# A decoder layer with routed experts on one core: the second group's expert choice, ranks and places moved earlier in the hand-written order

## The chip, the cores and the metric

The kernel runs on one core of one Trainium2 chip. The metric is the device time of one execution in microseconds (us), lower is better. TensorE is called PE, VectorE DVE, ScalarE ACT, GpSimd POOL and SyncE SP.

## The reference

The input `x` is 32 sequences of 64 tokens, 128 wide, so 2048 tokens. Three steps follow one another, each with a residual and a layer norm.

```python
x = layernorm(x + attention(x))            # 16 heads, causal, with a null key and value
x = layernorm(x + cross(x, ctx))           # per sequence: mean correlation -> top 8 delays,
                                           # softmax weights, shifted values summed, @ Wo.T
logits = x @ Wr + br                       # 8 experts
idx, gate = argmax(logits), max(softmax(logits))
h = gelu(x @ W1[idx] + b1[idx])            # 128 -> 512, exact gelu
x = layernorm(x + gate * (h @ W2[idx] + b2[idx]))
```

Every token goes through one expert alone, so the kernel has to know a token's expert before it can do the last layer of that token.

## The kernel before, in words

The 2048 tokens are 16 tiles of 128. A loop over the 16 steps runs the attention: in step t PE makes the scores of tile t+1 (L535), turns the probabilities of tile t (`turn_probs`), multiplies tile t-1's by the values (`mix_values`, L566) and projects tile t-2 out (`project_out`, L585). ACT takes the turned tiles out of PSUM, DVE subtracts maxima, normalises tile t-1 (`normalize`, L1057) and adds the residual of tile t-2 (`residual`, L1070), POOL masks the keys and multiplies the null values.

The cross attention and the choice of expert go by groups of four tiles. The four groups are tiles 0 to 3, 4 to 7, 8 to 11 and 12 to 15; in the tail of the program three of them are `g1, g2, g3` (g1 is the second group). `WHOLE` is g2, `NT` is 16. A group passes through this sequence, with the engine and the line of each step:

- `variance` and `inverse_std` give the first norm's scale (DVE L1157, POOL L411); `scale_routed` (L269) applies it to the routing columns; `means` (PE L662), `subtract_mean_max` (DVE L1170) and `exp_means` (ACT L934) give the delay weights; `first_norm` (ACT L915) the normed rows.
- `weight_sums` (DVE L1178), `taps`, `permute` (DVE L1184) and `circulants` (L286, POOL for g0 to g2) make a 128x128 matrix of each tile; `mix_context` (PE L676) multiplies the context values by it, in two parts of two tiles, and `second_sum` (DVE L1188) adds the rows to each.
- `square_sums` (ACT L922) and `second_inverse_std` (POOL L416) give the second norm's scale, `second_norm` (ACT L928) its rows.
- `logits` and `pick` (DVE L1197 and L1207, seven small operations) find the expert; `exp_logits` (ACT L938, eight small instructions for a group) sums the exponentials. `ranks` (PE L686) counts, with small matmuls into PSUM, where in its expert's region each token goes; `place` (DVE L1223) turns that into a row number and `gates` (DVE L1219) makes the gate, one reciprocal.
- `scatter` (POOL L429) writes the tile's rows to DRAM, sorted by expert, one indirect DMA for each tile.

After the scatters of the first 12 tiles have landed (`scattered_first`), SP loads the first 5 of 23 slots of 128 sorted rows (L362), and the last stage begins: for each slot PE turns the rows and runs both layers of its expert (`up`, L830, and `down`, L846), ACT the gelu, DVE the norm, POOL an inverse root and an indirect DMA to the output.

No planner sets the order; each engine's program is an order written out by hand, with waits on semaphores. In step 15, the last of the loop, DVE does: `normalize(14)`, `weight_sums(g2)`, `permute(g2)`, `residual(13)`, `logits(g1)`, `pick(g1)` (L1318 to L1363). Behind the loop each engine has a written tail: DVE L1368 to L1398, PE L799 to L814, ACT L975 to L989, POOL L483 to L490. POOL's tail is: two scatters of g1, `inverse_std(g3)`, `second_inverse_std(g2)`, the other two of g1, four of g2, `second_inverse_std(g3)`, four of g3. ACT's begins with the copy of tile 14's turned attention (`take_attnT`, L889), `exp_logits(g1)`, `first_norm(g2)`, the copy of tile 15's, and `square_sums(g2)` in two parts. A scatter waits for its group's places, gates and normed rows:

```python
pool.wait_ge(S["slots_ready"], g.n + 1)
pool.wait_ge(S["gate_ready"], g.n + 1)
pool.wait_ge(S["x2_ready"], g.first + g.size)
```

Of the kernel before, what the change touches and what calls it, by code (L numbers as in the profile page):

```python
# [18 lines left out]
NT = B * T // P  # L19
# [57 lines left out]
GROUPS = [Group(0, 0, 4), Group(1, 4, 4), Group(2, 8, 4), Group(3, 12, 4)]  # L77
WHOLE = GROUPS[2]
# [10 lines left out]
def due(step, lag):  # L89

    return [g for g in GROUPS if g.ready + lag == step]


def due_mixed(step, lag):

    return [g for g in GROUPS if g.mixed_at + g.more + lag == step]
# [11 lines left out]

def chosen_in(step):

    return due_mixed(step, 1) if step < NT - 2 else due_mixed(step, 2) if step == NT - 1 else []


def placed_in(step):
# [9 lines left out]
def decoder_layer(nc, a, out):  # L124
    with ExitStack() as ctx:
# [383 lines left out]
        def _(pe):  # L509
# [68 lines left out]
            def turn_attn(t):  # L578
                pe.wait_ge(S["attn_ready"], t + 1)
                pe.wait_ge(S["v_ready"], min(t + 5, NT))  # L580
                if t >= 1:
                    pe.wait_ge(S["attnT_ready"], t)
                nc.tensor.transpose(attnT_ps, attn[:, t % 2, :], ident).then_inc(S["attnT_done"], 1)
# [92 lines left out]
            def mix_context(g, k, done):  # L676

                if alone(g.mixed_at) and k == 0:
                    pe.wait_ge(S["y2_a_ready"], g.n)
                pe.wait_ge(S["cw_ready"], -(-(g.first + g.size) // CHUNK))  # L680
                pe.wait_ge(S["circ_ready"], g.n + 1)
                for j, t in enumerate(range(g.part(k).start, g.part(k).stop)):
                    last = nc.tensor.matmul(mix_ps(g, k)[:, j * EXT:(j + 1) * EXT], circ[:, t, :], cw[:, t, :], start=True, stop=True)
                last.then_inc(S[done], 1)
# [29 lines left out]
            def sixth_bank_read(t):  # L714

                made = {0: ("folds1_ready", 4), 1: ("folds2_ready", 2), 2: ("sk_ready", 1), 3: ("x_route_ready", 1), 4: ("a_route_ready", 1),
                        5: ("bias_ready", 1)}
                if t in made:
                    name, count = made[t]
                    pe.wait_ge(S[name], count)  # L720
                if 1 <= t < NT + 1:
                    pe.wait_ge(S["attn_ready"], t)
                for g in due(t, 1):
                    pe.wait_ge(S["m_sub"], g.n + 1)
                for g in first_mixed_in(t):
                    pe.wait_ge(S["y2_a_ready"], g.n + 1)
                for g in second_mixed_in(t):
                    pe.wait_ge(S["y2_b_ready"], g.wide_before + 1)
                for g in placed_in(t):
                    pe.wait_ge(S["ranks_taken"], g.n + 1)  # L730
# [67 lines left out]

            g1, g2, g3 = BEHIND  # L799
            turn_attn(NT - 2)  # L800
            sixth_bank_read(NT - 1)
            mix_values(NT - 1)
            ranks(g1)
            project_out(NT - 2)
            mix_context(g2, 0, "mix_a_done")
            turn_attn(NT - 1)
            mix_context(g2, 1, "mix_b_done")
            project_out(NT - 1)
            means(g3)
            ranks(g2)  # L810
            mix_context(g3, 0, "mix_a_done")
# [205 lines left out]
        def _(dve):  # L1017
# [283 lines left out]
            for t in range(NT):  # L1301
                for g in due(t, 2):
                    if t < NT - 1:
                        weight_sums(g)
                        permute(g)
                if t + 3 < NT:
                    rope(t + 3)
                if t == 2:
                    dve.wait_ge(S["late_consts_in"], 16)
                    v.tensor_copy(tri_b, const("earlier"))  # L1310
                    v.memset(ones_f[:, :], 1.0)
                    v.memset(jump_base[:, :], float(REGION))
                    v.memset(ones_b, 1.0)
                    v.tensor_copy(region_b.rearrange("p (t e) -> p t e", e=E), const("region_part").unsqueeze(1).to_broadcast([P, 4, E])).then_inc(S["ranks_in"], 1)
                if t + 1 < NT:
                    subtract_max(t + 1)
                sixth_bank_written(t)
                if t >= 1:  # L1318
                    normalize(t - 1)
                for g in due(t, 2):  # L1320
                    if t == NT - 1:
                        weight_sums(g)
                        permute(g)
                if t == 0:
                    weight_folds()
                if t == 1:
                    centered_folds()
                if t == 2:
                    context_keys()
                if t == 3:  # L1330
                    route_of_x()
                if t == 4:
                    route_of_attn()
                if t == 5:
                    query_bias()
                for g in due(t, 1):
                    subtract_mean_max(g)
                for g in first_mixed_in(t):
                    second_sum(g, 0, "mix_a_done", g.n + 1, "y2_a_ready")
                for g in second_mixed_in(t):  # L1340
                    second_sum(g, 1, "mix_b_done", g.wide_before + 1, "y2_b_ready")
                for g in placed_in(t):
                    place(g)
                if t == 2:
                    dve.wait_ge(S["x_all_in"], 16)
                    dve.wait_ge(S["x_zeros"], 1)
                if routed_in(t):
                    dve.wait_ge(S["routed_done"], t - routed_at(0) + 1)
                if t >= 2:
                    residual(t - 2)  # L1350
                if routed_in(t):
                    take_routed(t)
                for g in due(t, 0):
                    variance(g)
                for g in due(t, 1):
                    shifts(g)
                for g in placed_in(t):
                    gates(g)
                if t == 5:
                    dve.wait_ge(S["router_in"], 16)  # L1360
                for g in chosen_in(t):
                    logits(g)
                    pick(g)  # L1363
                if t < 2:
                    context_sums(2 * t)
                    context_sums(2 * t + 1)

            g1, g2, g3 = BEHIND  # L1368
            normalize(NT - 1)
            place(g1)  # L1370
            second_sum(g2, 0, "mix_a_done", g2.n + 1, "y2_a_ready")
            gates(g1)
            residual(NT - 2)
            second_sum(g2, 1, "mix_b_done", g2.wide_before + 1, "y2_b_ready")
            residual(NT - 1)
            variance(g3)
            scale_routed(dve, v, g3)
            shifts(g3)
            subtract_mean_max(g3)
# [126 lines left out]
```

## Time and profile before

| | |
|---|---|
| three runs, median (lowest to highest) | 195.6 us (195.48 to 199.49) |
| the profiled execution | 197.22 us |
| its span, first to last instruction | 195.4 us |
| mean granted TensorE clock in it | 0.918 |
| busy: PE, DVE, POOL, ACT | 157.0, 142.3, 110.3, 94.4 us |
| attention loop, by the timeline | to about 113 us |
| choice and placement of the rest | about 113 to 137 us |
| expert stage | about 137 us to the end |

Times in the views count from the first instruction of the span. The clock is given as a share: 1.00 is 2.4 GHz and 0.50 is 1.2 GHz. In the timeline a row is the start, the duration, the engine, the line, the operation and its tiles, and in square brackets how long the engine had sat idle and what released it. In the chain "issue" is time in which nothing of the profile shows what was waited for. Instructions of one engine overlap a little, since one is started before the last of the one ahead is written.

### The profile page before, as it was taken

What the parts mean: (1) busy time and instruction counts of PE and PEld (TensorE: products, weight loads), DVE (VectorE), ACT (ScalarE), POOL (GpSimd) and SP (SyncE); (2) the same over time, 40 slices, a digit from 0 to 9 for tenths busy, and PEclk for the clock granted to TensorE, in tenths of its full rate; (3) what the DMA queues carried; (4) which work ended last, traced back from release to release, by engine and by line L of the source; (5) the groups of instructions that cost most, each with busy time, mean ns of one, the idle gap of its engine ahead of it and who ended that gap; (6) DMA issues with size and microseconds to landing.
All of it is one profiled execution on the core that took longest, in us unless ns stands there. A gap on an engine that the chain in (4) does not pass through costs nothing.

```text
span 195.4 us, 5548 instructions
## 1 busy us (share of the span) xinstructions
PE 157.0 (80%) x1883; PEld 127.8 (65%) x1883; DVE 142.3 (73%) x493; ACT 94.4 (48%) x337; POOL 110.3 (56%) x149
## 2 busy tenths in 40 slices
PE   3999988899999899988798774260999999999800
PEld 1456765676678566765666664250899899999800
DVE  2567999968699598989768775784546588877850
ACT  3133335414441375239824573656656576766400
POOL 4524334365324563394386726673726689898982
PEclk9999999999999999999999988555589999999965
DMA  3699999999000000000000000015838977860100
GB/s 94 153 292 324 417 409 411 409 360 392 32 0 0 3 7 0 3 0 3 0 31 3 31 0 27 31 44 141 248 95 224 298 185 226 181 198 30 32 1 0
DMA packets 13035, 26.07 MB, mean 133 GB/s; under 512 B 2492, under 2 KB 7104, under 8 KB 11728
## 3 DMA queue, kind: packets, MB, share of 16 engines
q1 hardware_dynamic: 11760, 23.60, 37.4%
q0 software_dynamic: 1248, 2.12, 3.1%
q8 instruction: 16, 0.26, 0.5%
q14 instruction: 11, 0.09, 0.1%
HBM read 14.47 MB, written 11.69 MB: 134 GB/s over the span
## 4 chain that ended last, share of the span: by engine, by line
PE 40%; POOL 19%; issue 15%; ACT 13%; DVE 5%; DMA 4%; POOLq 1%; SPq 0%; DVEq 0%
POOL out L498 8%; POOL z_rstd L494 7%; PE ps L574 7%; ACT probsT L886 6%; PE ps L563 6%; PE ps L552 5%; PE ps L517 5%; PE ps L545 3%; POOL token_rows L435 2%; PE ps L649 2%; PE ps L842 2%; DMA token_rows<-rows,slots 2%; ACT v_blocks L878 1%; ACT lex L942 1%; ACT rows L932 1%
## 5 line engine op out<-in xcount | busy, mean ns | idle before, releaser
L886 ACT ACTIVATE probsT<-ps 128x512 f32<-128x512 f32 x32 | 19.1, 597 | 49.5 <-PE ps L563 49.1
L399 POOL TENSOR_TENSOR k<-qkT,consts 128x512 f32<-128x512 f32 x16 | 16.7, 1041 | 39.7 <-ACT qkT L878 39.7
L1001 ACT ACTIVATE gelT<-ps,w 128x128 f32<-128x128 f32 x92 | 26.5, 368 | 15.6 <-PE ps L842 15.6
L1044 DVE TENSOR_REDUCE row_max<-ps 128x16 f32<-128x1040 f32 x16 | 19.8, 1238 | 10.7 <-PE ps L552 10.7
L498 POOL DMA_INDIRECT out<-g_rows x23 | 24.3, 1057 | 4.4 <-issue 4.4
L842 PE MATMUL ps<-gxT,w 128*128 128x128 f32 x184 | 26.2, 289 | 0.0
L853 PE MATMUL ps<-w,gelT 128*128 x184 | 24.9, 280 | 0.3 <-ACT gelT L1001 0.3
L842 PEld LDWEIGHTS ps<-gxT,w 128*128 128x128 f32 x184 | 24.1, 204 | 0.2 <-ACT gxT L878 0.2
L435 POOL DMA_INDIRECT token_rows<-rows,slots x16 | 16.1, 1005 | 13.8 <-issue 8.8
L853 PEld LDWEIGHTS ps<-w,gelT 128*128 128x128 f32 x184 | 23.0, 196 | 0.7 <-issue 0.7
L1053 DVE TENSOR_TENSOR probs<-ps,row_max 128x512 f32<-128x512 f32 x32 | 21.9, 686 | 1.5
L563 PE MATMUL ps<-consts,probs 128*128 128x128 f32 x128 | 19.8, 277 | 3.7 <-ACT probsT L886 2.9
L574 PEld LDWEIGHTS ps<-v_blocks,probsT 128*64 128x64 f32 x512 | 16.3, 138 | 6.9 <-issue 6.9
L563 PEld LDWEIGHTS ps<-consts,probs 128*128 128x128 f32 x128 | 14.4, 140 | 6.8 <-issue 3.6
L574 PE MATMUL ps<-v_blocks,probsT 128*64 128x18 f32 x512 | 17.8, 212 | 1.1 <-issue 0.6
L494 POOL TENSOR_TENSOR z_rstd<-z_rstd,consts 128x1 f32<-128x1 f32 x23 | 13.9, 603 | 7.2 <-DVE z_rstd L1427 6.6
L517 PE MATMUL ps<-wqk,xT 128*128 128x256 f32 x32 | 12.8, 487 | 3.4 <-DMA wqk<-in_wqk 3.4
L1407 DVE TENSOR_TENSOR z<-ps,b_bc 128x128 f32<-128x128 f32 x23 | 6.7, 291 | 10.4 <-PE ps L853 6.2
L391 POOL TENSOR_TENSOR roped<-roped,rope_b 128x128 f32<-128x128 f32 x16 | 7.3, 457 | 11.6 <-DVE rope_b L1036 11.6
L552 PE MATMUL ps<-k,qkT 32*64 32x260 f32 x256 | 12.1, 435 | 0.0
L878 ACT ACTIVATE qkT<-ps 128x256 f32<-128x256 f32 x16 | 6.2, 384 | 9.3 <-PE ps L531 9.2
L1416 DVE TENSOR_SCALAR g_rows<-z,z_mv,z_rstd 128x128 f32<-128x128 f32 x23 | 8.3, 359 | 2.9 <-POOL z_rstd L494 1.3
(188 smaller groups left out, 330.7 us busy)
## 6 DMA issues: line engine op xcount, KB each, us to landing
token_rows<-g_rows SPq DMA_DIRECT2D x8, 1105.0 KB, 13.2
w<-in_w SPq DMA_DIRECT2D x23, 258.0 KB, 3.3
w<-in_w SPq DMA_DIRECT2D x1, 2048.0 KB, 22.0
g_rows<-token_rows SPq DMA_DIRECT2D x23, 65.0 KB, 3.1
ctxT<-in_ctxT SPq DMA_DIRECT2D x1, 1024.0 KB, 7.6
xT<-in_xT SPq DMA_DIRECT2D x3, 256.0 KB, 5.0
b_bc<-in_b SPq DMA_DIRECT2D x1, 512.0 KB, 22.2
out<-g_rows POOLq DMA_INDIRECT x23
```

What stands on the lines that cost most here:

```text
L435: pool.indirect_dma_start(out=rows_dram, out_offset=bass.IndirectOffsetOnAxis(ap=slots[:, t:t + 1], axis=0), in_=rows[:, t, :], in_offset= ...
L494: nc.gpsimd.tensor_tensor(z_rstd[:, n % 2, 1:2], z_rstd[:, n % 2, 0:1], const("minus_half")[:, 0:1], ALU.pow).then_inc(S["z_rs"], 1)
L498: pool.indirect_dma_start(out=out, out_offset=bass.IndirectOffsetOnAxis(ap=g_rows[:, n, D + 1:D + 2].bitcast(U32), axis=0), in_=g_rows[:, ...
L517: nc.tensor.matmul(proj_ps(t), xT[:, t, :], wqk[:, :], start=True, stop=True).then_inc(S["proj_done"], 1)
L552: last = nc.tensor.matmul(ps[b * T:(b + 1) * T, s, 0:HPS * KW], qkT[rows_s, r, b * T:(b + 1) * T], k4[rows_s, r, b, :, :].rearrange("p h k ...
L563: last = nc.tensor.transpose(turned_ps[:, (c % 4) * P:(c % 4 + 1) * P], probs[:, r, c * P:(c + 1) * P], ident)
L574: last = nc.tensor.matmul(ps[b * T:(b + 1) * T, 6, PAIR * c:PAIR * (c + 1)], probsT[:, r, c, b * T:(b + 1) * T], v_blocks[:, t % 4, at:at ...
L842: last = nc.tensor.matmul(hT_ps(n % 2, c), w1[:, n % RING, c * P:(c + 1) * P], gxT[:, n % 2, :], start=True, stop=True)
L853: last = nc.tensor.matmul(y_ps(n % 2), gelT[:, n % 2, c * P:(c + 1) * P], w2[:, bass.ds(e * (FC * D) + c * D, D)], start=(c == 0), stop=(c ...
L886: nc.scalar.activation(probsT[:, t % 2, 4 * half:4 * half + 4, :].rearrange("p a b -> p (a b)"), turned_ps, ACT.Exp, scale=SCALE).then_inc ...
L1001: last = nc.scalar.activation(gelT[:, n % 2, c * P:(c + 1) * P], ps[:, 2 * (n % 2) + c // 2, (c % 2) * P:(c % 2 + 1) * P], ACT.Gelu, bias= ...
L1053: v.tensor_tensor(probs[:, r, 512 * half:512 * half + 512].rearrange("p (s h k) -> p s h k", h=HPS, k=T), strips_ps[:, 2 * half:2 * half + ...
```

## The change

In step 14, DVE's program gets `weight_sums(g2)` at its end. In step 15, right behind `normalize(14)`, it gets `logits(g1)` and `pick(g1)`, and `permute(g2)` follows them. At the end of step 15 it gets `place(g1)` and `gates(g1)`, which so stand ahead of `normalize(15)`. In DVE's tail `second_sum(g2, 1)` goes behind `residual(15)` and `variance(g3)`. In PE's tail `ranks(g1)` goes ahead of `mix_values(15)`, and `project_out(15)` ahead of `mix_context(g2, 1)`. ACT's, POOL's and SP's programs are as they were, and no operation is added or removed.

```diff
--- before.py
+++ after.py
@@ -108,7 +108,7 @@
 
 def chosen_in(step):
 
-    return due_mixed(step, 1) if step < NT - 2 else due_mixed(step, 2) if step == NT - 1 else []
+    return due_mixed(step, 1) if step < NT - 2 else []
 
 
 def placed_in(step):
@@ -798,14 +798,14 @@
 
             g1, g2, g3 = BEHIND
             turn_attn(NT - 2)
+            ranks(g1)
             sixth_bank_read(NT - 1)
             mix_values(NT - 1)
-            ranks(g1)
             project_out(NT - 2)
             mix_context(g2, 0, "mix_a_done")
             turn_attn(NT - 1)
+            project_out(NT - 1)
             mix_context(g2, 1, "mix_b_done")
-            project_out(NT - 1)
             means(g3)
             ranks(g2)
             mix_context(g3, 0, "mix_a_done")
@@ -1317,10 +1317,10 @@
                 sixth_bank_written(t)
                 if t >= 1:
                     normalize(t - 1)
-                for g in due(t, 2):
-                    if t == NT - 1:
-                        weight_sums(g)
-                        permute(g)
+                if t == NT - 1:
+                    logits(GROUPS[1])
+                    pick(GROUPS[1])
+                    permute(WHOLE)
                 if t == 0:
                     weight_folds()
                 if t == 1:
@@ -1361,19 +1361,22 @@
                 for g in chosen_in(t):
                     logits(g)
                     pick(g)
+                if t == NT - 2:
+                    weight_sums(WHOLE)
+                if t == NT - 1:
+                    place(GROUPS[1])
+                    gates(GROUPS[1])
                 if t < 2:
                     context_sums(2 * t)
                     context_sums(2 * t + 1)
 
             g1, g2, g3 = BEHIND
             normalize(NT - 1)
-            place(g1)
+            residual(NT - 2)
             second_sum(g2, 0, "mix_a_done", g2.n + 1, "y2_a_ready")
-            gates(g1)
-            residual(NT - 2)
-            second_sum(g2, 1, "mix_b_done", g2.wide_before + 1, "y2_b_ready")
             residual(NT - 1)
             variance(g3)
+            second_sum(g2, 1, "mix_b_done", g2.wide_before + 1, "y2_b_ready")
             scale_routed(dve, v, g3)
             shifts(g3)
             subtract_mean_max(g3)
```

## Rows read from the trace of the kernel before

**Rows 1.** The page, the span in 40 equal slices: granted TensorE clock in tenths

```profile
PEclk9999999999999999999999988555589999999965
```

**Rows 2.** The chain that ended last, 108 to 150 us: start us, us, what

```profile
113.67 4.43 issue
...
118.87 1.01 POOL token_rows L435
...
121.15 1.06 POOL rstd L414
...
122.48 1.03 POOL rstd L421
...
124.20 1.25 ACT lex L942 x8
...
131.32 3.36 DMA token_rows<-rows,slots
```

**Rows 3.** Line 1201 alone: ns min/median/max, first and last start us

```profile
L1201 DVE TENSOR_TENSOR lg<-y,rstd x4: 174/193/1247, 89.6 to 133.8; 128x32 f32<-128x32 f32 x4
```

**Rows 4.** Timeline, 96 to 114 us: start us, us, engine, line, tiles

```profile
99.96 0.73 PE L683 MATMUL ps<-cw,circ 128*128 128x136 f32 x4
...
109.01 0.22 ACT L936 ACTIVATE w_tok<-w_tok 128x32 f32<-128x32 f32 x1
...
110.46 0.32 DVE L1063 TENSOR_TENSOR ps<-ps,null_v 128x144 f32<-128x144 f32 x1 [1.10 <-PE ps L574]
...
111.00 0.43 POOL L407 TENSOR_TENSOR null_v<-null_e,vnull 128x144 f32<-128x144 f32 x1
...
111.11 0.29 DVE L1067 TENSOR_TENSOR attn<-ps,rden 128x128 f32<-128x128 f32 x1
...
111.62 0.39 DVE L1186 TENSOR_REDUCE w_perm<-w_taps 128x32 f32<-128x256 f32 x1
...
112.40 1.27 POOL L294 TENSOR_TENSOR circ<-consts,w_norm 128x512 f32<-128x512 f32 x1
112.47 1.25 DVE L1201 TENSOR_TENSOR lg<-y,rstd 128x32 f32<-128x32 f32 x1
...
113.09 1.11 PE L574 MATMUL ps<-v_blocks,probsT 128*64 128x18 f32 x32 [0.62 <-issue]
```

**Rows 5.** Timeline, 114 to 128 us (as group 4)

```profile
114.87 0.19 DVE L1217 TENSOR_TENSOR onehot<-eqr,first 128x32 bf16<-128x32 f32 x1
...
115.35 1.63 ACT L919 ACTIVATE x<-y_all,shift,rstd 128x128 f32<-128x128 f32 x4
...
117.84 0.17 DVE L1221 RECIPROCAL rows<-lsum 128x4 f32<-128x4 f32 x1
...
118.36 0.80 PE L597 MATMUL ps<-wo_route,attnT 128*128 128x152 f32 x2
...
119.34 0.32 DVE L1075 TENSOR_TENSOR y_all<-ps,x_all 128x152 f32<-128x152 f32 x1 [0.29 <-PE ps L598]
...
120.43 0.17 DVE L1163 TENSOR_SCALAR var_eps<-mv 128x4 f32<-128x4 f32 x1
...
127.50 0.96 POOL L435 DMA_INDIRECT token_rows<-rows,slots  x1 [1.50 <-ACT rows L932]
```

**Rows 6.** Windows: stretch, us, PE busy (instructions), granted clock, DMA share, GB/s

```profile
114.00:115.00 1.00, 0.43 (x12) 1.00 0.00 0
...
116.00:117.00 1.00, 1.00 (x6) 0.50 0.00 0
...
142.00:143.00 1.00, 1.00 (x7) 0.53 0.82 258
```

**Rows 7.** Timeline, 137 to 144 us: first-layer matmuls of two slots

```profile
137.83 2.08 PE L842 MATMUL ps<-gxT,w 128*128 128x128 f32 x8
...
143.26 1.06 PE L842 MATMUL ps<-gxT,w 128*128 128x128 f32 x8
```

**Rows 8.** Windows: stretch, us, busy PE, PEld, DVE, ACT, POOL, clock, DMA, GB/s

```profile
170.00:180.00 10.00, 10.00 (x92) 10.00 (x91) 7.90 (x33) 7.08 (x28) 8.79 (x11) 1.00 0.47 126
```


## The prediction, made before the changed kernel ran

> **What bounds the kernel now.** I read the page first, then the chain of waits, then the timeline of step 15 and the tail. The slices of the granted clock [rows 1] show three stretches: an attention loop at full clock, a middle with low digits from about 112 to 142 us, and an expert stage at full clock. The middle is the placement of the remaining tokens, in which PE is mostly idle. The chain of waits there [rows 2] runs through POOL: the first scatter of g1 at 118.87, the root for g3 at 121.15, the root for g2 at 122.48, g2's exponentials at 124.20, then g2's scatters, whose last lands 3.36 us after 131.32, and with it the expert stage may begin. In front of 118.87 the chain shows 4.43 us of "issue" behind a DVE `lg` of g1. That is g1's choice working its way through places and gates to POOL's first scatter. POOL's order is fixed, so everything behind that scatter is late with it: the root for g3 could start at 120.60, when `var_eps` is written (120.43 + 0.17) [rows 5], and starts at 121.15 because two scatters of g1 stand ahead. So two things set the start of g2's root: the late scatters, and right behind them tile 15's own residual and variance.
>
> **Step 14: weight sums of g2 moved forward.** Two small DVE operations, about 0.4 us. Their input is written by ACT at 109.01 + 0.22 = 109.23, and DVE sat idle for 1.10 us before 110.46 [rows 4]. They fit in that gap: cost nothing. Without that cover, 0.4 us on DVE.
>
> **Step 15: choice of g1 ahead.** `lg` took 1247 ns here and 174 to 193 elsewhere [rows 3], and it ran from 112.47 to 113.72 beside POOL's `circ`, which ran from 112.40 to 113.67 [rows 4]. I read it as blocked by `circ`. Now `lg` follows `normalize(14)`, which ends at 111.40, and what POOL has running is the null values until 111.43, so it loses at most the rest of that. The seven operations took from 112.47 to 115.06 (114.87 + 0.19) [rows 4, 5]; of this 1.25 is `lg` and 1.34 the rest. New: 111.4 to about 112.9. The onehots come 2.1 us earlier. If the long `lg` were not a matter of `circ` it would cost 1.05 more; I take zero, because the others of the line agree within 0.02.
> The Trainium skill, page "SBUF — State Buffer", section "Who interferes with whom", says that a DVE instruction with two SBUF inputs and a GpSimd one that reads SBUF exclude each other for the whole instruction, and that one SBUF input doesn't contend. This trace agrees (1247 ns beside `circ`). By the rule the DVE work that falls beside `circ` in the new order (residual, places, gates) isn't slowed; with a lock of any two it would be late by up to 1.27 us.
>
> **`permute(g2)` behind the choice.** `w_perm` moves from 111.62 to about 112.85, so `circ` from 112.40 to 113.65, ending at 114.9 instead of 113.67 [rows 4]. Its reader is `mix_context(g2, 0)`, which PE reaches at about 115.0 (below), so it costs 0; if PE came at once, up to 0.5.
>
> **PE: ranks of g1 ahead of the last values.** The early part of the ranks and the turn of tile 14 are done by 112.8; the onehots at 112.9 let the rest go, 0.25 us. `mix_values(15)` then starts at 113.25 instead of 113.09 (1.11 long) [rows 4] and ends at 114.35. `project_out(14)` no longer waits for the onehots (115.06 before): about 114.4 to 115.0. `mix_context(g2, 0)`: 115.0 to 115.7, by the 0.73 us of this line at full clock [rows 4].
>
> **DVE: places and gates ahead of `normalize(15)`.** `residual(13)` ends at 113.8, `place` at 114.2. The gates wait for ACT: the exponentials now start behind tile 14's copy at 113.2 and take 1.25 [rows 2], so to 114.45. Gates 0.17 [rows 5]: written at 114.65. That wait holds up `normalize(15)` and all behind it on DVE; but its values are only ready at 114.35, so it costs 0.3. Before, it stood behind the onehots, which were written at 115.06. Now it ends at 115.55 (0.94 us, as tile 14's from 110.46 to 111.40 [rows 4]). Behind it wait `residual(14)`, both sums and PE's turn of tile 15.
>
> **ACT.** `first_norm(g2)` took 1.63 [rows 5]: now 114.5 to 116.1. Tile 15's copy follows it, to 116.4. PE has turned the tile by 116.05, so ACT is the later.
>
> **`project_out(15)` ahead of `mix_context(g2, 1)`.** Before it began at 118.36 at half clock (0.80 for its first part) [rows 5]. Now 116.45 to 117.0 at full clock. `residual(15)` and `variance(g3)` took 1.26 together (119.34 to 120.60 [rows 5]): now 117.05 to 118.3. So `var_eps` of g3 is 2.3 earlier.
>
> **POOL.** `circ` to 114.9, two scatters of g1 (2.3 us with the gap, [rows 2]) from about 115.7 to 118.0. They no longer stand in the way: the root for g3 runs from 118.35 to 119.4, where it ended at 122.21.
>
> **The second half of g2's sum, moved back.** PE does it at 117.0 to 117.7, DVE behind the variance to 118.75, ACT squares until 119.45. POOL is through with g3's root at 119.4, so this is a tie: next late is this sum of squares. g2's root then needs 0.2 + 1.03 plus gaps [rows 2]: it ends at 120.85 instead of 123.50. **Gain 2.65 us.**
>
> **Behind it.** The other two scatters of g1 follow to 123.2; g2's scatter waited for ACT's normed rows at 127.50 [rows 5] and now does so at about 124.9, so they are covered. From g2's root to the landing at 134.68 nothing changes: exponentials, rows, four scatters, landing. Everything there, the weight loads of SP too, moves as one. The expert stage has PE busy for 10.00 of 10 us and POOL for 8.79 in one of its stretches [rows 8], and its length doesn't hang on its start. So the gain carries to the end, less 0 to 0.3 for gaps and semaphores that I set at nothing. I take 2.6.
>
> **Sum.** The profiled execution took 197.22 us, 1.8 more than its span; 197.22 - 2.6 = 194.6. The median of the three runs is 195.6, 1.6 below that execution. The same 2.6 off gives **193.0 us**.
>
> **What the clock does.** The granted clock is 1.00 at 114 to 115, 0.50 at 116 to 117 [rows 6], after a us in which PE was busy for 0.43. In the new order PE has more to do there, so I let it stay at 2.4 GHz. If it falls all the same, PE's four pieces from 115.6 on (0.7, 0.3, 0.55, 0.7 at full clock) take twice that; `project_out(15)` then ends at 117.65, the squares at 120.15, g2's root at 121.5: gain 2.0. If the squares slip behind still further, with a late start of the second mix, 1.2. The Trainium skill, "TensorE: Matmul & The Clock Gate", Part 1, says that activity releases the clock and that the point of the change varies from run to run. No row here shows the variation. By it a run of the kernel before may have kept its clock in this stretch; then its end is about 0.7 earlier, and the change brings 2.0 against it.
>
> **The rivals.**
> 1. *Half the gain.* The clock stays low at 116, or the squares of g2 or the ACT copy are later than I think. For it: the tie above, and ACT's serial 1.25 + 1.63. Against: PE's idle time goes. Gain 1.0 to 2.0, time 193.6 to 194.6.
> 2. *More than the forecast.* The expert stage starts at half clock: eight matmuls took 2.08 at 137.83 and 1.06 at 143.26 [rows 7], and the clock came back inside 142 to 143 [rows 6]. If it returns 0.8 to 1.6 us earlier, counted from the start of the stage, half of that, 0.4 to 0.8, is added: 192.2 to 192.6.
> 3. *Absorbed.* The start of the expert stage is set by something not on this path, say weight loads, or POOL loses at the end what it gained. For it: POOL nearly full late in the stage [rows 8]. Against: a full engine that starts earlier ends earlier. 195.4 to 195.8.
> 4. *The other side: the clock comes back later.* The expert stage begins earlier, but PE is granted half clock for much longer in it, because its short pieces in the middle now leave a longer quiet piece. At half clock eight matmuls lose 1.02 of 2.08, so each us at 1.2 GHz costs about 0.5. Against a gain of 2.6 it decides from 5.2 us more of low clock; with 8 us more it is 195.6 + 4 - 2.6 = 197.0. For it: about 20 us in a row at 0.50 or 0.53 before. Against: PE works without a gap from 137.8 on.
> 5. *It doesn't do what it says.* ACT's exponentials start late, the gates' wait holds `normalize(15)` back, and POOL's first scatter comes behind 117.5. Then gain under 1, time 194.8 to 195.6. ACT's free time at 113.2 to 114.2 speaks against it.
>
> **Chances.** Forecast (192.6 to 193.6) 0.52, rival 1 0.2, rival 2 0.09, rival 3 0.08, rival 4 0.05, rival 5 0.06. I leave out rival 4 and the edges of 2: range 192.2 to 195.5. By the bound of 2%, about what a measurement of this kernel can tell from no change, faster means under 191.7, slower over 199.5. All cases but tails lie within: faster 0.05, same 0.93, slower 0.02.
>
> **What would show it.** In the profile after: `lg` of g1 near 0.2 us at 111.4; `circ` ending near 114.9; the first scatter of g1 at 115.7; the root of g3 at about 118.4 with no scatter directly ahead of it; the root of g2 ending at about 120.9 and its release by ACT's squares; the first load of rows at about 132.1 instead of behind 134.68; the clock at 1.00 through 116 to 119; the first up-matmuls at 135.2. The prediction is wrong if the root of g2 ends behind 122.3, or if it is early and the end isn't.

## The result, and the profile after

| | kernel before | changed kernel |
|---|---|---|
| median of 13 runs (lowest to highest) | 198.59 us (195.48 to 202.41) | 197.51 us (192.96 to 201.68) |
| profiled execution, and its span | 197.22, 195.4 us | 197.24, 195.4 us |
| two further comparisons, 12 runs of the changed kernel each | 196.98 and 197.28 us | 194.25 and 195.28 us |

The ratio of the changed kernel to the one before is 0.990 (95% interval 0.985 to 0.995), and 0.991 (0.987 to 0.995) and 0.991 (0.986 to 0.996) when it was measured again. The ratios leave out runs more than 1.5% above the fastest of their kernel, and by the medians of all runs the three are 0.995, 0.986 and 0.990. So the change takes off some 1.0%, about 1.9 us. Forecast were 1.3%, but as a time 193.0 us with a range to 195.5: the measured median of 197.5 lies outside. Both kernels' runs spread over 7 to 9 us, and the three runs known at the time of the forecast were a low draw of them. In the two further comparisons the changed kernel's medians, 194.25 and 195.28, lie inside the range, so the level moves from one comparison to the next.

The two profiled executions have the same span. The change is to be seen only if one counts from a common point. The timeline of step 15 of the changed kernel:

```profile
112.38 0.32 DVE L1063 TENSOR_TENSOR ps<-ps,null_v 128x144 f32<-128x144 f32 x1 [1.18 <-PE ps L574]
...
113.22 0.18 DVE L1201 TENSOR_TENSOR lg<-y,rstd 128x32 f32<-128x32 f32 x1
...
114.56 0.19 DVE L1217 TENSOR_TENSOR onehot<-eqr,first 128x32 bf16<-128x32 f32 x1
114.67 0.41 DVE L1186 TENSOR_REDUCE w_perm<-w_taps 128x32 f32<-128x256 f32 x1
...
115.48 1.27 POOL L294 TENSOR_TENSOR circ<-consts,w_norm 128x512 f32<-128x512 f32 x1
...
116.91 1.01 POOL L435 DMA_INDIRECT token_rows<-rows,slots  x1 [0.16 <-issue]
...
118.07 0.88 PE L597 MATMUL ps<-wo_route,attnT 128*128 128x152 f32 x2 [0.37 <-ACT attnT L878]
...
119.03 1.25 PE L683 MATMUL ps<-cw,circ 128*128 128x136 f32 x4
...
120.33 0.17 DVE L1163 TENSOR_SCALAR var_eps<-mv 128x4 f32<-128x4 f32 x1
```

Its chain of waits:

```profile
116.07 0.69 POOL circ L294
...
116.90 0.70 PE ps L683 x4
...
117.74 0.28 ACT attnT L878
...
118.07 0.88 PE ps L597 x2
...
120.59 1.04 POOL rstd L414
...
122.06 1.02 POOL rstd L421
```

`normalize(14)` starts at 112.38 here and at 110.46 in [rows 4]. From there `lg` begins 0.84 us later and takes 0.18 instead of 1.25 [rows 4]; the first scatter comes at 4.53 instead of 8.41 [rows 2]; g2's root ends at 10.70 (123.08) instead of 13.04 (123.50). That is 2.34 us. But this execution was 1.92 us late by the start of `normalize(14)`. 1.08 of it is there already at the first exp (next section). The other 0.84 arises in the loop: from the first exp to `normalize(14)` it took 93.19 here and 92.35 in the kernel before. The only thing that the change has there is g2's two weight sums, and they aren't the cause: two more executions of the changed kernel took 92.35 and 92.37, and e2 below, which doesn't have them, took 93.16. So the weight sums cost nothing, as forecast. The chain no longer has the 4.43 us of "issue" [rows 2]: POOL waits for nothing but g3's `var_eps` now, and that path goes back through project_out(15), ACT's copy and the first mix to `circ`.

### The profile page after: what moved, and what is told of

It is laid out like the page before. It is cut to its first block, busy times and chain, and to the rows that moved or that the text cites. A ratio compares the mean times of both kernels' runs of the same rounds, so it can differ in the third digit from the quotient of the medians.

```text
span 195.4 us, 5548 instructions
## 1 busy us (share of the span) xinstructions
PE 157.7 (81%) x1883; PEld 128.3 (66%) x1883; DVE 141.6 (72%) x493; ACT 94.2 (48%) x337; POOL 110.6 (57%) x149
## 4 chain that ended last, share of the span: by engine, by line
PE 42%; POOL 19%; ACT 14%; issue 13%; DVE 6%; DMA 1%; POOLq 1%; SPq 1%; DVEq 0%
POOL out L498 8%; POOL z_rstd L494 7%; PE ps L574 7%; ACT probsT L886 6%; PE ps L563 6%; PE ps L552 5%; PE ps L517 5%; PE ps L545 3%; PE ps L649 2%; PE ps L842 2%; ACT rows L932 2%; ACT lex L942 2%; PE ps L683 2%; POOL token_rows L435 2%; ACT v_blocks L878 1%
## 5 line engine op out<-in xcount | busy, mean ns | idle before, releaser
L1044 DVE TENSOR_REDUCE row_max<-ps 128x16 f32<-128x1040 f32 x16 | 19.8, 1238 | 12.2 <-PE ps L552 12.2
L563 PE MATMUL ps<-consts,probs 128*128 128x128 f32 x128 | 20.3, 282 | 4.1 <-ACT probsT L886 3.5
L1053 DVE TENSOR_TENSOR probs<-ps,row_max 128x512 f32<-128x512 f32 x32 | 21.9, 686 | 1.5
L517 PE MATMUL ps<-wqk,xT 128*128 128x256 f32 x32 | 13.3, 504 | 3.5 <-DMA wqk<-in_wqk 3.3
L1410 DVE TENSOR_TENSOR z<-ps,b_bc 128x128 f32<-128x128 f32 x23 | 6.7, 291 | 10.4 <-PE ps L853 5.8
## 6 DMA issues: line engine op xcount, KB each, us to landing
w<-in_w SPq DMA_DIRECT2D x1, 2048.0 KB, 21.9
```

The source lines that it names most:

```text
L517: nc.tensor.matmul(proj_ps(t), xT[:, t, :], wqk[:, :], start=True, stop=True).then_inc(S["proj_done"], 1)
L563: last = nc.tensor.transpose(turned_ps[:, (c % 4) * P:(c % 4 + 1) * P], probs[:, r, c * P:(c + 1) * P], ident)
L1053: v.tensor_tensor(probs[:, r, 512 * half:512 * half + 512].rearrange("p (s h k) -> p s h k", h=HPS, k=T), strips_ps[:, 2 * half:2 * half + ...
```

## Where the runs spread

The late start is there from the first microseconds on. The first exp of step 0's probabilities, in the timeline of the kernel before:

```profile
18.11 0.60 ACT L886 ACTIVATE probsT<-ps 128x512 f32<-128x512 f32 x1 [3.31 <-PE ps L563]
```

and of the kernel before once more (b2), where it is the latest of all:

```profile
9.03 1.17 PE L552 MATMUL ps<-k,qkT 32*64 32x260 f32 x16
...
14.28 1.17 PE L552 MATMUL ps<-k,qkT 32*64 32x260 f32 x16
...
19.20 0.60 ACT L886 ACTIVATE probsT<-ps 128x512 f32<-128x512 f32 x1 [4.54 <-PE ps L563]
...
21.41 0.69 PE L552 MATMUL ps<-k,qkT 32*64 32x260 f32 x16
```

The same sixteen matmuls take 1.17 us at 9.03 and 14.28 and 0.69 at 21.41: PE is at 1.2 GHz first, at 2.4 GHz later. The clock column reads 1.00 there, since it knows no event before the first; the durations tell it. The first entry of the trace's clock record is the rise itself: it stands at 16.65 us in the kernel before and at 20.86 in b2, and at 19.11, 15.06 and 12.54 in the three executions of the changed kernel. The first exps of these five come in the same order. In the execution of a3_same_third:

```profile
16.29 0.60 ACT L886 ACTIVATE probsT<-ps 128x512 f32<-128x512 f32 x1 [2.09 <-PE ps L563]
```

In the table, "first exp" is that row, the first result of step 0's probabilities on ACT. "Part" is from the start of `normalize(14)` to the end of g2's root (L421), "rest" the span minus the first exp. "Clock falls" is where the granted clock goes to 0.50, counted from `normalize(14)`.

| execution | span | first exp | part | clock falls | rest |
|---|---|---|---|---|---|
| before | 195.4 | 18.11 | 13.04 | 5.2 | 177.3 |
| before again (b2) | 197.6 | 19.20 | 13.19 | 4.3 | 178.4 |
| changed | 195.4 | 19.19 | 10.70 | 5.7 | 176.2 |
| changed again (a2) | 193.2 | 17.35 | 11.37 | 4.4 | 175.9 |
| changed, third (a3) | 191.3 | 16.29 | 10.25 | 9.7 | 175.0 |

One kernel has spans from 191.3 to 195.4, and 2.9 of these 4.1 us lie ahead of the first exp. By the rest, which leaves that piece out, the changed kernel is 2.2 us shorter in the mean (175.7 against 177.9), of three executions and two. The part is 1.7 to 2.9 shorter, and how much depends on the clock.

## The experiments

The diffs are against the changed kernel where nothing else is said, and shortened.

**a2, a3, b2: the same kernels again.**

> The changed kernel once more, nothing edited. Theory (the middle is 2 us shorter in every execution, and what spreads the runs over 8 us is how long PE stays at 1.2 GHz after the first matmul): from normalize(14) to the end of g2's root 10.6 to 11.3 us again; the first exp of step 0's probabilities starts anywhere from 16.2 to 19.2 us, by the matmul durations before it; ratio 0.987 to 0.993. Rival (the 2 us in the middle were luck of one profile): over 12 us there, ratio 0.997 to 1.003.

> The changed kernel a third time, beside the next two on the same chip. Theory: ratio 0.987 to 0.994; span minus the start of step 0's first exp is 175.5 to 176.5 us, whatever that start is.

> The kernel before once more, nothing edited. Theory (the spread of the runs comes from the start, where PE stays at 1.2 GHz for a varying time): the matmuls of L552 ahead of step 0 take 1.17 or 0.69 as the case may be, the first exp of step 0 starts between 15 and 19.2 us (18.11 in the profile before), and what follows it takes 176.9 to 177.8 us (177.3 there). Rival (the spread arises all along the span): the part behind that point differs by over 1 us.

The gain came back: 11.37 and 10.25 in the part, ratios 0.991 twice. 11.37 is a little over the expected 11.3, 175.0 a little under 175.5. b2's rest of 178.4 is over the expected 177.8 because the low clock went on into step 0: its next step took 5.74 us, 5.18 to 5.19 in the others. So most of the spread lies at the start, and some in the middle: one step of the loop takes 6.31 us in some executions and 6.74 in others, in either order (6.74 in e2), and the granted clock falls at a different point of the middle in each.

**e3: `permute(g2)` ahead of the choice.**

```diff
+                    permute(WHOLE)
                     logits(GROUPS[1])
                     pick(GROUPS[1])
-                    permute(WHOLE)
```

> The changed kernel with permute(g2) ahead of g1's choice in step 15, as before, so that POOL's circ runs beside the choice. Theory (DVE operations with two SBUF inputs are held until circ ends): one of the seven operations of the choice, lg or eqr, takes 0.9 to 1.3 us instead of 0.19; the onehots come 1.3 to 1.6 us later and mix_values(15) with them; 11.5 to 12.2 us from normalize(14) to g2's root, ratio 0.995 to 1.000. Rival (the long lg had another cause, and the earlier circ helps): no operation over 0.3 us, 10.3 to 10.7 us.

DVE's and POOL's timeline of e3:

```profile
110.58 0.18 DVE L1201 TENSOR_TENSOR lg<-y,rstd 128x32 f32<-128x32 f32 x1
110.80 0.23 DVE L1203 TENSOR_TENSOR lg<-lg,br_bc 128x32 f32<-128x32 f32 x1
111.06 0.19 DVE L1205 TENSOR_REDUCE lmin<-lg 128x4 f32<-128x32 f32 x1
111.28 1.09 DVE L1211 TENSOR_TENSOR eqr<-lg,lmin 128x32 f32<-128x32 f32 x1
```

```profile
111.06 1.27 POOL L294 TENSOR_TENSOR circ<-consts,w_norm 128x512 f32<-128x512 f32 x1
```

`lg` is free now, because `circ` hasn't begun. `eqr` starts beside it and isn't through until `circ` ends at 112.33. The reduction at 111.06, with one input, isn't held. So the stall belongs to `circ` and falls on whichever operation with two SBUF inputs comes during it. That is the rule of the Trainium skill, "SBUF — State Buffer", "Who interferes with whom", and this run agrees with it in what is held and in what is not. The part took 13.50 us, more than the expected 11.5 to 12.2. The late onehots hold the last values back on PE, and these then run at 1.2 GHz (1.90 instead of 1.11): the clock had fallen 3.9 us behind `normalize(14)`. The ratio is 1.007 (0.998 to 1.017). All of the gain is gone.

**e7: ranks, places and gates late again.**

```diff
             sixth_bank_read(NT - 1)
             mix_values(NT - 1)
+            ranks(g1)
...
-                if t == NT - 1:
-                    place(GROUPS[1])
-                    gates(GROUPS[1])
...
             normalize(NT - 1)
+            place(g1)
+            second_sum(g2, 0, "mix_a_done", g2.n + 1, "y2_a_ready")
+            gates(g1)
             residual(NT - 2)
-            second_sum(g2, 0, "mix_a_done", g2.n + 1, "y2_a_ready")
```

> The changed kernel with g1's ranks again behind the last values, its places behind normalize(15) and its gates behind the first sum of g2, as in the kernel before; the choice stays early and the tail's swaps stay. Theory (POOL's two scatters of g1 must be through before g3's var_eps is written): the first scatter starts 6.2 to 6.8 us after normalize(14) instead of 4.53, the two end 0.2 to 0.8 behind var_eps, and g2's root ends at 10.9 to 11.5 instead of 10.70; ratio 0.990 to 0.996. Rival (earlier places and gates are what makes the gain): root at 12.2 or later, ratio near 1.000.

POOL's timeline of e7, in which `normalize(14)` starts at 108.88:

```profile
115.52 1.01 POOL L435 DMA_INDIRECT token_rows<-rows,slots  x1 [2.26 <-issue]
116.83 0.97 POOL L435 DMA_INDIRECT token_rows<-rows,slots  x1 [0.31 <-issue]
117.80 1.06 POOL L414 TENSOR_TENSOR rstd<-var_eps,consts 128x4 f32<-128x4 f32 x1
```

g3's `var_eps` was written at 116.90, and the root could start only at 117.80, behind the scatters: 0.9 us. The first scatter is 6.64 behind `normalize(14)`, the part is 11.27, both as expected. The clock held until 9.9 us there, so a3 is the one to compare, with 10.25: early ranks, places and gates carry 1.0 us. The ratio of 0.998 (0.991 to 1.005) is over the expected 0.990 to 0.996, but its interval overlaps that.

**e1 and e2: the two swaps of the tail, undone and alone.** In e1 `mix_context(g2, 1)` stands ahead of `project_out(15)` again and its sum ahead of `residual(15)`; e2 is the kernel before with these two swaps only.

> The change without its two swaps in the tail: g1's choice, ranks, places and gates early, but the second mix of g2 again ahead of project_out(15) on PE and its sum again ahead of residual(15) on DVE. I count from the start of normalize(14) (L1063) to the end of g2's root (L421): 13.04 us in the kernel before, 10.70 in the changed one. Theory (each part carries its share, project_out(15) is on the path): project_out(15) starts 0.5 to 0.9 us later than in the changed kernel, so 11.2 to 11.6 us, and 0.992 to 0.997 of the kernel before. Rival (the swaps are covered by ACT's copy of tile 15): 10.7 us and 0.990.

> The kernel before with only the two swaps in the tail. Theory (g3's root is held by the two late scatters of g1, so an earlier residual(15) is worth nothing alone): 12.9 to 13.1 us from normalize(14) to the end of g2's root, ratio 1.000. Rival (the swaps bring most of the gain): under 12.4 us and under 0.995.

e1 gave a part of 11.30 and 0.995 (0.987 to 1.003), e2 12.22 and 0.991 (0.982 to 1.000). By these numbers e1 speaks for my theory and e2 for the rival. But the medians of all ten runs give 0.990 for e1 and 1.002 for e2, the other way round, and in the profiles the clock mixes in. e1's clock fell 4 us behind `normalize(14)`; the changed kernel, when it fell at 4.4 (a2), took 11.37, no less than e1. In e2 it held until 6.2, the first mix took 0.71 us instead of 1.25, and the first scatter, which stands ahead of the swaps' effect, came at 7.59 instead of 8.41. These 0.82 us are all by which the part is shorter. So what the swaps bring is under what these runs can tell, and e2 rather shows the price of the clock.

**e4 and e12: the choice in step 14, in DVE's 1.18 us of waiting** (one kernel, run twice).

```diff
                 if t == NT - 1:
-                    logits(GROUPS[1])
-                    pick(GROUPS[1])
                     permute(WHOLE)
...
                     weight_sums(WHOLE)
+                    logits(GROUPS[1])
+                    pick(GROUPS[1])
```

> The changed kernel with g1's logits and pick moved further, to the end of step 14 behind g2's weight sums, where DVE waited 1.18 us for the values. Theory (circ behind the choice now holds the first mix of g2, whose PE start was released by circ): circ ends 0.8 to 1.3 us sooner after normalize(14), project_out(15) starts 0.3 to 0.8 sooner; 10.0 to 10.4 us from normalize(14), whose own start may slip 0.4; ratio 0.985 to 0.990. Rival (ACT's exponentials and first norm of g2 set tile 15's copy, not circ): 10.6 to 10.8 us and 0.990 to 0.992.

> The kernel e4_choice_in_14 once more, unchanged, for a narrower interval: it gave 0.9867 with 0.967 to 1.007. Theory (it saves circ's wait, some 0.5 us over the changed kernel, if the clock holds): ratio 0.984 to 0.990; from normalize(14) to g2's root 9.9 to 10.5 us where the clock is at 1.00 until the end of project_out(14). Rival (no more than the changed kernel): 0.990 to 0.993.

0.987 (0.967 to 1.007) from four runs, then 1.002 (0.996 to 1.008) from twelve: no gain, and probably a loss against the changed kernel. The part was 9.92 in e12, as expected, but 11.24 in e4, where the clock fell 1.5 us ahead of `normalize(14)` already. And `normalize(14)` itself came late: 93.74 us behind the first exp in e12 and 94.51 in e4, where a2 and a3 have 92.35 and 92.37. So in e12 the later start takes back what the shorter part gives. From g2's root to the end e4's profile took 70.9 us, 1.0 less than any other; the cause isn't known. DVE's and POOL's timeline of e12:

```profile
108.99 0.65 DVE L1203 TENSOR_TENSOR lg<-lg,br_bc 128x32 f32<-128x32 f32 x1
109.68 0.19 DVE L1205 TENSOR_REDUCE lmin<-lg 128x4 f32<-128x32 f32 x1
109.90 0.39 DVE L1211 TENSOR_TENSOR eqr<-lg,lmin 128x32 f32<-128x32 f32 x1
110.32 0.35 DVE L1213 TENSOR_TENSOR eqr<-eqr,consts 128x32 f32<-128x32 f32 x1
```

```profile
109.07 0.49 POOL L427 TENSOR_TENSOR cw<-cw,bvo 128x136 f32<-128x136 f32 x1
109.50 0.73 POOL L282 TENSOR_TENSOR w_taps<-w_tok,consts 128x256 f32<-128x256 f32 x1
110.20 0.42 POOL L407 TENSOR_TENSOR null_v<-null_e,vnull 128x144 f32<-128x144 f32 x1
```

Each of the three long DVE rows ends within 0.1 us of the end of one on POOL. The idle time of DVE was no free time: POOL was busy in it. The choice took 2.35 us there, and 1.53 in the changed kernel; 1.53 alone would already have been 0.35 more than the wait that was to hide it.

**e5 and e10: PE kept busy in the middle.**

```diff
+            def keep_busy(n):
+
+                for _ in range(n):
+                    nc.tensor.matmul(ps[:, 7, 0:480], ident_b, cb[:, 0:480], start=True, stop=True)
```

It is called with 6 ahead of `means(g3)`, 5 and 16 ahead of the onehots of g2 and g3, 6 ahead of g3's first mix and 3 ahead of the first turned rows. e10 is e5 with the POOL swap of e11.

> The changed kernel with 36 bf16 matmuls of 128x480 put into PE's waits of the middle (ahead of g3's means, of the onehots of g2 and g3, of g3's first mix and of the first turned rows). Their results go to a bank that nothing reads. Theory (the expert stage's first two slots run at 1.2 GHz because PE was idle before): the clock stays at 1.00 through most of the middle and the eight first matmuls take 1.06 instead of 2.08; first root of the expert stage 2 to 2.6 us sooner after the first up matmul (7.0 us in the changed kernel); 1.5 to 2.5 us off the end, ratio 0.977 to 0.984. Rival (loads of weights or POOL set the pace of the first slots): matmuls at 1.06 but the end not over 0.5 us earlier, ratio 0.987 to 0.991.

> The kernel with 36 matmuls in PE's waits (e5_busy_tail), and g3's second root ahead of g2's fourth scatter. Theory (with the clock up, the first slots have 2 to 3 us to spare, and g3's rows alone bind): load of slot 5's rows 1.0 to 1.3 us sooner after g2's root than in e5_busy_tail (21.6 us there), the end 1 to 2.5 us before that kernel's, ratio 0.985 to 0.996. Rival (the 36 matmuls hurt in a way of their own): ratio over 1.000.

e5: 1.005 (1.000 to 1.011), slower than theory and rival had it; e10: 0.996 (0.990 to 1.002), at the upper edge of what theory gave. In e5 the part was 10.23. But the matmuls didn't do what they were put in for. The granted clock was 1.00 until 133.0 and fell just as the first slot began, so its eight matmuls were as slow as before. The first slot's root came 6.37 us behind the first up matmul, where the changed kernel has 6.99, 6.00 (a2) and 7.46 (a3). So e5 tests neither the theory nor the rival. What it shows is a wait of PE behind the fourth slot's first layer. Its timeline in e5:

```profile
133.14 2.07 PE L851 MATMUL ps<-gxT,w 128*128 128x128 f32 x8 [0.53 <-ACT gxT L888]
...
142.71 0.33 PE L837 MATMUL ps<-consts,g_rows 128*128 128x128 f32 x1 [2.06 <-DMA g_rows<-token_rows]
```

The last row is the turn of slot 5's rows, the first of the later slots. It needs g3's scatters, and PE has it ahead of slot 2's second layer. PE was free for it 21.9 us behind g2's root, and in a2 21.5 us behind it, so it was not early in e5. The rows were late: SP began to load them 4.0 us behind the start of the last scatter, and 3.0 to 3.3 us behind it in the three executions of the changed kernel. The clock fell once more at 143.3, for 3.4 us. So e5 loses its time at slot 5; why the rows came late, and whether the added matmuls have a part in it, is not shown. In e10 the first eight matmuls did take 1.09 us, but then the clock was at 0.50 from 134.3 to 141.1. The load of slot 5's rows came 20.4 us behind g2's root, 1.2 sooner than in e5, the end came 73.4 us behind it instead of 75.2, and the ratio fell by 0.009, between two chips. e11, which is e10 without the matmuls, has 0.991 on e10's chip: the matmuls brought no gain there either.

**e11: g3's second root ahead of g2's fourth scatter.**

```diff
-            scatter(g2, g2.tiles)
+            scatter(g2, g2.tiles[:3])
             second_inverse_std(g3)
+            scatter(g2, g2.tiles[3:])
```

> The changed kernel with g3's second root on POOL ahead of g2's fourth scatter instead of behind it. In ten profiles the third slot's root follows g2's root by 25.7 to 26.3 us however early the first slot was, since PE turns the first row of the later slots (it needs g3's scatters) ahead of the third slot's second layer. Theory (the expert stage is bound by g3's rows, the first slots have under 1 us to spare): g3's root 1.25 us sooner, the first slots 1.3 us later, the end within 0.6 us of the changed kernel's, ratio 0.988 to 0.994. Rival (the first slots' path alone sets the end): 1.3 us later than the changed kernel, ratio near 0.997.

> The kernel e11_root_ahead once more, unchanged, beside the changed kernel on the same chip. Theory (it trades 1.3 us of the first slots' spare time for 1 us of g3's rows): its ratio is 0.003 to 0.006 under the changed kernel's. Rival (a tie, as in the first two calls): within 0.002.

0.991 (0.986 to 0.996), then 0.984 (0.977 to 0.991), beside 0.991 of a3 on the same chip. From g2's root to the end it took 72.4 us in both profiles; the changed kernel took 72.3, 72.1 and 72.4. So g3's root 1.1 us sooner bought nothing in the profiles. Most of it was gone before the rows were loaded: the last scatter began 16.4 us behind g2's root instead of 17.6, but SP's load of slot 5's rows 20.4 behind it instead of 20.6 to 20.9, since the wait for the scatter's landing was longer (4.0 and 3.9 us from the scatter's start). Whether the 0.007 of the second comparison is real stays open: the intervals overlap.

**e8: matmuls ahead of the first load.**

```diff
+            pe.wait_ge(S["warm_made"], 1)
+            for _ in range(5):
+                nc.tensor.matmul(ps[:, 3, :], warm[:, 0:P], warm[:, :], start=True, stop=True)
             pe.wait_ge(S["wqk_in"], 16)
             project(0)
             project(1)
+            nc.tensor.matmul(ps[:, 3, 0:256], warm[:, 0:P], warm[:, 0:256], start=True, stop=True)
...
+            v.memset(warm[:, :], 1.0).then_inc(S["warm_made"], 1)
```

> The changed kernel with 5 bf16 matmuls of 128x512 on PE ahead of the first projection, in the 3.4 us in which it waits for the first load, and a sixth of 256 columns behind project(1), their operand set by a DVE memset. Theory (the length of the low-clock piece at the start spreads the runs): the matmuls of L552 in step -1 and 0 take 0.69 instead of 1.17, the first exp of step 0 starts at 15.5 to 16.5 us, the spread of the timed runs shrinks from 8 us to under 6, and the median falls by 1 to 2 us against the changed kernel's. Rival (the point is not moved by what PE does there): first exp again anywhere from 16.2 to 19.2, spread and median as before.

> The kernel e8_busy_start once more, unchanged, for 10 to 12 runs instead of 6. Theory (the matmuls ahead of the first projection bring the clock up sooner): the first exp of step 0 at 15 to 16.3 us again and a median 1 to 2 us under the changed kernel's of the same call. Rival (the chance of the phase sets it, and the 15.30 of the first profile was one of its values): first exp anywhere from 15.3 to 19.2 us, medians within 0.7 us.

The first exp in the two profiles is at 15.30 and 15.29 us. The second:

```profile
15.29 0.60 ACT L891 ACTIVATE probsT<-ps 128x512 f32<-128x512 f32 x1 [2.08 <-PE ps L564]
```

Without these matmuls it was between 15.67 and 19.20 in fifteen profiles. The clock record's first entry stands at 5.40 and 5.89 us, and the sixteen matmuls take 0.70 us from the first time on. The ratio is 0.989 (0.982 to 0.995) and 0.984 (0.979 to 0.988), the medians 194.19 and 193.93 us, beside 194.25 and 195.28 for the changed kernel beside them. The first comparison fits the rival (medians within 0.7 us), the second the theory. So the start got shorter and steadier, and e8 is at least as fast as the changed kernel; by how much isn't settled. In the second comparison it is level with e11 as the fastest here (0.984 both). The spread didn't shrink as I expected (192 to 199.5 us still), so the start is not all of it. Both its profiles lose some of the gain at slot 5, as e5 did:

```profile
142.53 0.47 PE L833 MATMUL ps<-consts,g_rows 128*128 128x128 f32 x1 [2.53 <-DMA g_rows<-token_rows]
```

From g2's root to the end they took 74.7 and 75.3 us. SP began to load those rows 5.0 and 4.8 us behind the start of the last scatter, 3.1 in the kernel before and 3.3 in a3. Over all seventeen profiles this distance goes from 2.7 (b2) to 5.0. Why the landing is later there I don't know.

## Why the prediction was right and wrong

**Wrong: the level.** The step that failed is "The same 2.6 off gives 193.0 us". It took the median of three runs, 195.6, as the kernel's level. Thirteen runs gave 198.59; the changed kernel's thirteen gave 197.51, 4.5 us over the forecast, while the difference was forecast as 2.6 and measured as about 1.9. The warning was on the table, 195.48 to 199.49 and a profiled execution 1.6 over the median, and I used it for nothing. The spread comes largely from how long PE runs at 1.2 GHz at the start (1.17 against 0.69 for the same matmuls), which the row of the clock doesn't show: the first exp varies by 3.5 us over fifteen profiles without e8's matmuls.

**Right: the mechanism, in its order and mostly in size.** Counted from `normalize(14)`, forecast and changed kernel: onehots 2.4 and 2.37, end of `circ` 4.4 and 4.37, last values 2.8 and 2.62, start of project_out(15) 6.0 and 5.69, g3's `var_eps` 7.8 and 8.12, g3's root 8.9 and 9.25, g2's root 10.4 and 10.70. The profiles in which the clock held through project_out(15) (a3, e5, e10, both of e8, the first of e11) all have 10.22 to 10.25. `lg` took 0.18. The tie that was forecast is there to within 0.02: ACT's squares of g2 ended at 121.61 and g3's root at 121.63, and g2's root followed. The first scatter came sooner than forecast, 4.53 instead of 5.2, and that gained nothing, since POOL then waited for `var_eps`. The order that e3 undid and the early places that e7 undid each carry part of the gain, as the steps say. For the two swaps of the tail this isn't shown (e1, e2).

**The clock.** I let it stay at 2.4 GHz. It fell in the changed kernel 5.7 us behind `normalize(14)`, at the start of project_out(15) (0.88 for its first part), and the part was 10.70 instead of the 10.22 to 10.25 with the clock held; in a2 it fell at 4.4 and the part was 11.37. I had put 11.04 to that case (a gain of 2.0). It also fell late in one execution of the kernel before's order (e2), and then the part was 12.22, where I had said "about 0.7 earlier" than 13.04. So the two prices were near, 0.15 us too long with the clock held and 0.3 too short without it, and it was the certainty that was wrong: the piece at half clock moves from run to run, in either kernel, and the mean gain, about 1.9 us by the ratio, lies nearer to the 2.0 without the clock than to 2.6.

**Carrying to the end.** "Its length doesn't hang on its start" held, for another reason than the one I gave. From g2's root to the end it is 71.9 and 72.3 us in the kernel before and 72.1 to 72.4 in the changed one. I had followed the first scatters and the first slots. There is a second path of nearly the same length, through g3's rows for slot 5: PE waits 0.23 us for them in the changed kernel, 0.93 in a2 and not at all in a3. Where they come late (e5, e8), everything behind is late. Both paths go through g2's root, so the sum came out right. In eight of the first ten profiles the third slot's root follows g2's by 25.7 to 26.3 us, whether the first slot's follows by 20.4 or 21.8. The other two, e5 and e8, have 28.1 and 28.4, which my expectation for e11 left out.

**The rivals.** Rival 1, half the gain, is nearest to the mean that was measured, and by its own first cause, the clock. Rival 2's thought, that an earlier return of the clock in the expert stage adds to it, isn't borne out: in a2 the clock came back 16.9 us behind g2's root and in the kernel before 19.4, the first slot's root came 1.2 us sooner, the third's 0.3, and the end not sooner (72.1 and 71.9). e5, which was to test it, didn't: its first slot ran at half clock all the same. Rivals 3 and 5 didn't occur: the gates' wait cost nothing (DVE went from the places at 115.95 straight to the gates). Rival 4 was not seen. By the bound of 2% the result is no change, as forecast.

## What to carry to other kernels

Before a time is forecast, look how far the runs of one kernel lie apart and give the range that width; here the ratio was known within 0.5%, 1 us, while the kernel before had medians from 195.6 (three runs) to 199.3 (25 runs). Compare two profiles from a common instruction near the change, not by their spans. A place in an order is free only if the other engine of a shared port is idle too: moving a chain of small DVE operations from beside one long POOL operation took 1.07 us off them, and moving it into DVE's own idle time, beside three POOL operations, put 0.8 on. Before an experiment is read, look whether its edit did its work: e5's matmuls were to keep the clock up for the first slot, and it fell as that slot began.

## What the runs showed of the hardware that I had not expected

- The clock of TensorE at the start: five bf16 matmuls of 128x512 from 1.45 us on, while PE waited for its first load, and a sixth of 256 columns put the first exp at 15.30 and 15.29 us, and without them it was anywhere from 15.67 to 19.20. The Trainium skill, "TensorE: Matmul & The Clock Gate", Part 1, says that the point varies from run to run; the fifteen profiles agree. Behind the start the loop is steady: nine of its fifteen steps agree within 0.03 us in all seventeen profiles, one takes 6.31 in some and 6.74 in others, and the other five are longer in one or two profiles.
- Matmuls put into TensorE's waits don't have to bring anything: with 36 of them the clock stayed at 1.00 until 133.0, fell as the first slot began, and fell again at 143.3, after PE had idled 2.06 us for slot 5. The ratio was 1.005, and 0.991 without them.
- Landing of the last scatter: SP's load, which waits for it, began 2.7 to 5.0 us behind the scatter's start. In one kernel run three times it was 3.0 to 3.3, with e8's matmuls and their operand's memset 5.0 and 4.8. The cause is open.
